# Gated cross-attention block with a quantized feed-forward: three global maxima turned by TensorE, unread matmuls ahead of the gate and down products, their first tiles worked together

## The chip, the cores and the metric

The kernel runs on one core of one Trainium2 (trn2) chip. The metric is the device time of one execution in microseconds (us), as the median of several runs; a time is better when it is lower. A change of 0.3% is about 5.7 us here.

## What is computed

The reference is a two-part transformer block on `x` of shape (4, 1024, 512): a gated cross-attention with 16 heads of 32 columns, and a gated feed-forward (512 to 1536 and back) whose weights and activations are rounded to integer grids. Only the second part matters for this change:

```python
def act_qdq(x):
    qmax = 32767.0
    scale = jnp.maximum(jnp.max(jnp.abs(x)) / qmax, 1e-12)
    return jnp.clip(jnp.round(x / scale), -qmax - 1.0, qmax) * scale

x = act_qdq(x)
up = act_qdq(x @ lpbq_dequant(w_up).T)
gate = act_qdq(x @ lpbq_dequant(w_gate).T)
sig = fixed_qdq_u16(jax.nn.sigmoid(gate))
gate = act_qdq(gate * sig)
o = act_qdq(gate * up)
return o @ lpbq_dequant(w_down).T
```

Every `act_qdq` takes one maximum over a whole tensor of 4096 rows, and nothing behind it can be rounded before that maximum is known. So the feed-forward is a row of stages with a global maximum between each two.

## The kernel before, in words

Five programs run side by side, one for each engine's queue: `sync_program` (SP, all DMAs but a few), `tensor_program` (PE), `scalar_program` (ACT), `vector_program` (DVE) and `gpsimd_program` (POOL). They meet at semaphores only. Each program is written out in order; what an engine does next is the next line of its program, and it waits there if a semaphore is not yet high enough.

The first part (up to about 998 us) is the attention, cut into steps by `all_steps`. The change touches one line of it: `aggregate` (L1391), which turns the statistics of the last batch's rows into means and variances. POOL makes the standard deviations from them (`deviation_2`, L1729), and DVE the largest normalized value of all rows, "x_row" (L1492).

A global maximum is made by `everywhere` (L1326). Each partition holds its own maximum in one column. DVE spreads that column over 32 columns (L1329), turns the four 32x32 blocks (L1332), and reduces the turned rows into four blocks of partitions (L1335): nine DVE instructions, and every partition then holds the largest value. The names are listed at L272. `quant_scale` (L1477) makes the scales from it.

Then come these stages of the feed-forward:

- **x tiles.** 32 tiles of 128 rows are centred, scaled and split into a high and a low fp16 part: `centre_x` (L1293) and `quant_x` (L1498) on DVE, `high_x` (L1147) on ACT, `low_x` (L1504) on DVE, and a transposing DMA into `x_hl` by `turn_x` (L680) on SP. The first 8 tiles are made before the gate product starts; the others beside it, at units given by `x_tile` (L203).
- **gate.** 48 units (4 column parts of 1024 rows, `cp`, by 12 weight tiles, `ot`). `project` (L984) computes one unit: two halves `h` of 512 columns, 12 matmuls each, into one of four PSUM tiles (`quad`). The first unit of each `cp` waits before each half for the four x tiles of that half. ACT copies a unit out (`evict`, L1153) into one of three `ev` buffers; DVE takes its largest absolute value and its largest value (L1513, L1517); SP stores it. Beside that DVE also makes the x tiles of the next `cp` and rounds the weights of up and down (`TILE_JOBS`), all in the order of the units.
- **up.** 48 units more, while ACT and DVE work on the sigmoid of the gate. Then "u_row", the maximum of up.
- **product maximum.** 48 pieces; ACT takes two absolute values of each (L1208, L1222), DVE multiplies and reduces (L1608). PE has nothing to do. Then "o_row".
- **down.** 8 chunks `ch` of 512 rows. For each chunk and each of 12 `ot` the second operands are made (`make_o`, L1632: `quantize_up` on ACT, `make_oq` on DVE, `high_o` on ACT, `low_o` on DVE). PE then computes four output tiles of a chunk one after the other (L1009 to L1028), 36 matmuls each: 12 `ot` by 3 products. DVE adds the residual (L1652) and SP stores the tile (L864). The 12 operands of the first chunk are made before any output; those of chunk `ch + 1` beside the four tiles of chunk `ch`, three for each (L1644, and on SP L859 for their loads).

Of the kernel before, what the change touches and what calls it, by code (L numbers as in the profile page):

```python
# [6 lines left out]
ALU = mybir.AluOpType  # L7
ACT = mybir.ActivationFunctionType
AX = mybir.AxisListType
F32 = mybir.dt.float32  # L10
# [257 lines left out]

ALL = 9
ALL_NO = {n: ALL * (k + 1) for k, n in enumerate(("w0", "x_row", "w1", "w2", "g_row", "s_row", "h_row", "u_row", "o_row"))}  # L272


R1, R2 = 9, 9
# [19 lines left out]
class Kernel:  # L295


    def __init__(self, nc, ctx, x, ctx_in, gx, gf, wg, wu, wd, cos_d, sin_d, id_d, bias_d, out):
# [34 lines left out]
        self.ymax = A("ymax", [128, NT], F32)  # L333
        self.red = A("red", [128, 12], F32)
        self.spread = A("spread", [128, 32], F32)
        self.turned = A("turned", [32, 128], F32)
        self.qs = A("qs", [128, 24], F32)
        self.wmx = A("wmx", [128, 12], F32)
# [90 lines left out]
        def sem(name):  # L429
            return ctx.enter_context(nc.semaphore(name))  # L430
# [27 lines left out]
        self.pe_prj, self.pe_down = sem("pe_prj"), sem("pe_down")  # L458
# [28 lines left out]
    def bank_release(self, use, half):  # L487

        n = UNIT[use] - 2
        while n >= 0:  # L490
            kind, *a = UNIT_USES[n]
            if kind == "max":
                return self.v_max, max_no(*a)
            if kind == "out":
                return (self.v_x2 if half else self.v_rec), a[0] + 1
            if kind == "turn":
                return self.v_lo, turn_no(*a, half)
            if half == 0:
                return self.v_wl, w_no(*a)
            n -= 2  # L500
        return None

    def w_buffer(self, m, k):

# [59 lines left out]


TODO = [(ch, ot) for ch in range(NCH) for ot in range(OT)]

# [4 lines left out]
def sync_program(e, K):  # L572
# [253 lines left out]
    def load_o(n):  # L826
        ch, ot = TODO[n]
        load_up(ot, slice(512 * ch, 512 * ch + 512), 512)
# [25 lines left out]
    for ch in range(NCH):  # L854
        for i in range(4):
            m = 4 * ch + i
            if m + 1 < NT:
                load_xr(m + 1)
            if ch + 1 < NCH:  # L859
                for n in range(OT * (ch + 1) + 3 * i, OT * (ch + 1) + 3 * i + 3):  # L860
                    if n + NUF < len(TODO):
                        load_o(n + NUF)
# [9 lines left out]
def tensor_program(e, K):  # L872
# [108 lines left out]
        before = st  # L981


    def project(k, W, cp):  # L984
        z = k % 4
        for h in range(2):
            c0 = 1024 * cp + 512 * h
            if h == 0 and k >= 4:
                e.wait_ge(K.a_ev, k - 3)
            if k < 48 and k % OT == 0:  # L990
                for j in range(NXS):
                    e.wait_ge(K.d_xt[j], 16 * (c0 // 512) + 16)
            terms = [(0, c, c) for c in range(CC)] + [(0, c, CC + c) for c in range(CC)] + [(1, c, c) for c in range(CC)]
            for n, (part, c, x) in enumerate(terms):
                mm = e.matmul(K.quad[z][:, 512 * h:512 * h + 512], W(part, c), K.x_hl[:, x, c0:c0 + 512], start=n == 0, stop=n == 11)  # L995
        mm.then_inc(K.pe_prj, 1)

    e.wait_ge(K.a_den, NHALF)
    e.wait_ge(K.a_num, NHALF)
    e.wait_ge(K.d_Wg, 32)  # L1000
    for cp in range(4):
        for ot in range(OT):
            project(12 * cp + ot, lambda part, c: K.Wg[part][:, ot, 128 * c:128 * c + 128], cp)
    for ot in range(OT):
        e.wait_ge(K.d_Wu[ot % 2], 32 * (ot // 2) + 32)
        for cp in range(4):
            project(48 + 4 * ot + cp, lambda part, c: K.Wu[ot % 2][part][:, c, :], cp)

    for ch in range(NCH):  # L1009
        k = ch % 2  # L1010
        for i in range(4):
            n = 4 * ch + i
            z = n % 8
            ps = K.quad[z // 2][:, 512 * (z % 2):512 * (z % 2) + 512]
            sl = slice(128 * i, 128 * i + 128)
            if n == 0:
                e.wait_ge(K.a_ev, 96)
                e.wait_ge(K.d_Wd, 128)
            if n >= 8:
                e.wait_ge(K.v_out, n - 7)  # L1020
            m = 0
            for ot in range(OT):
                if i == 0:
                    e.wait_ge(K.v_ol, OT * ch + ot + 1)
                for o, r in ((K.oh, 0), (K.ol, 0), (K.oh, 1)):
                    mm = e.matmul(ps, o[k][:, ot, sl], K.Wd[r][:, ot, :], start=m == 0, stop=m == 3 * OT - 1)  # L1026
                    m += 1
            mm.then_inc(K.pe_down, 1)  # L1028

# [225 lines left out]
def vector_program(e, K):  # L1255
# [69 lines left out]

    def everywhere(out, column, name):  # L1326

        n = ALL_NO[name] - ALL
# [75 lines left out]
    for st in STEPS:  # L1404
# [45 lines left out]
        if st.stats is not None:  # L1450
            p, qc, part = st.stats
            g, c = p % 4, slice(4 * qc, 4 * qc + 4)
            if part == 0:
                if (p, qc) == (NQ - 1, 1):
                    e.wait_ge(K.v_x2b, 1)
                else:
                    e.wait_ge(K.g_x2, 2 * p + qc + 1)
                for i in range(4 * qc, 4 * qc + 4):
                    e.bn_stats(K.st2[:, i, g, :], K.x2s[:, i, :]).then_inc(K.v_st2, 1)
            else:  # L1460
                o, op = (K.rmx, ALU.max) if part == 1 else (K.rmn, ALU.min)
                e.tensor_reduce(o[:, c, g], K.x2s[:, c, :], AX.X, op).then_inc(K.v_st2, 1)
# [178 lines left out]
    for ch in range(NCH):  # L1641
        for i in range(4):
            m = 4 * ch + i
            if ch + 1 < NCH:  # L1644
                for n in range(OT * (ch + 1) + 3 * i, OT * (ch + 1) + 3 * i + 3):
# [221 lines left out]
```

## Time and profile before

| | us |
|---|---|
| median of 3 runs (lowest, highest) | 1890.52 (1889.78, 1894.19) |
| the profiled execution, its time | 1895.78 |
| the profiled execution, its span (first to last instruction) | 1894.0 |
| PE busy, share of the span | 1680.0, 89% |
| DVE busy | 1498.3, 79% |
| ACT busy | 1184.7, 63% |
| POOL busy | 809.7, 43% |

Busy times are sums over stages with different limits, so the shares say little about one stage. Times in rows count from the first instruction of the span. A row of the timeline reads: start, duration, engine, line, operation, output tile <- input tiles, shape of output <- input, count, and in brackets how long the engine was idle before it and what ended that. SPq is the DMA queue that SP feeds; its rows are the issues of DMAs, not their transfers. PEld is the load of a matmul's stationary operand. PEclk is the granted clock of TensorE as a share of 2.4 GHz: 1.00 is 2.4 GHz, 0.50 is 1.2 GHz, values between are means over a stretch in which it changed.

### The profile page before, as it was taken

To read this page: it belongs to the slowest core of one execution; us is meant where nothing else is said; L and a number is where in the kernel's file an instruction comes from. 1 tells how busy PE (TensorE), PEld (TensorE's weight loads), DVE (VectorE), ACT (ScalarE), POOL (GpSimd) and SP (SyncE) were. 2 spreads that over 40 slices of the span, in tenths; PEclk is the share of its full clock that TensorE was granted. 3 is DMA by queue.
4 is the path that set the end of the run, shared out by engine and by line. 5 is a ranking of instruction groups with operands and counts; after the bars stand their busy time and mean duration, and the time that the engine had idled before them with its cause. 6 is when DMAs were issued, how large, how long until landed. Compare 5 with 4: busy or idle time off the path is not lost. (4 is left out here: it accounts for less than half of the span.)

```text
span 1894.0 us, 24954 instructions
## 1 busy us (share of the span) xinstructions
PE 1680.0 (89%) x8888; PEld 632.1 (33%) x8888; DVE 1498.3 (79%) x2140; ACT 1184.7 (63%) x1898; POOL 809.7 (43%) x442
## 2 busy tenths in 40 slices
PE   2899999999999999999985999999999920399999
PEld 0223333333333333333222444444444400144444
DVE  6899888888888887888845998968889999855551
ACT  3476777777777777777662332329896689744440
POOL 4488888978889888887630010110000000000000
PEclk9899999999999999999997999999999965699999
DMA  5576777656776667766454888749993469755552
GB/s 157 142 177 155 182 178 185 145 141 140 182 180 139 166 141 177 170 140 139 86 167 129 251 259 245 231 156 267 281 280 131 139 213 291 250 175 167 168 172 72
DMA packets 234044, 339.49 MB, mean 179 GB/s; under 512 B 74400, under 2 KB 153120, under 8 KB 225664
## 3 DMA queue, kind: packets, MB, share of 16 engines
q1 hardware_dynamic: 224992, 272.89, 48.2%
q0 software_dynamic: 8928, 65.02, 17.2%
q8 instruction: 70, 1.15, 0.3%
q14 instruction: 54, 0.44, 0.1%
HBM read 164.04 MB, written 92.41 MB: 135 GB/s over the span
## 5 line engine op out<-in xcount | busy, mean ns | idle before, releaser
L1074 ACT ACTIVATE P<-quad 128x512 f32<-128x512 f32 x1024 | 557.3, 599 | 231.4 <-PE quad L913 227.1
L1271 DVE TENSOR_REDUCE cm<-quad 128x1 f16<-128x1024 f32 x512 | 601.1, 1216 | 86.3 <-PE quad L901 85.0
L1792 POOL TENSOR_TENSOR Ps<-P,P 128x2048 f32<-128x2048 f32 x93 | 422.8, 4546 | 153.8 <-ACT P L1074 153.7
L913 PE MATMUL quad<-QA,KA 101*128 101x512 f16 x1024 | 352.8, 385 | 7.5 <-ACT P L1074 6.4
L901 PE MATMUL quad<-KA,QA 100*128 100x512 f16 x1024 | 328.0, 391 | 27.1 <-DVE wh L1379 6.6
L1026 PE MATMUL quad<-Wd,oh 128*128 128x512 f16 x768 | 231.2, 381 | 113.7 <-DVE ol L1630 113.7
L949 PE MATMUL quad<-P,cg 128*32 128x512 f32 x2048 | 273.6, 606 | 3.5 <-ACT numT L1111 0.6
L995 PE MATMUL quad<-x_hl,Wg 128*128 128x512 f16 x1152 | 251.7, 382 | 23.1 <-DMA x_hl<-xs 22.9
L995 PE MATMUL quad<-x_hl,Wu 128*128 128x512 f16 x1152 | 250.7, 381 | 2.1 <-DMA Wu<-wt_scratch 2.1
L1158 ACT ACTIVATE ev<-quad 128x1024 f32<-128x1024 f32 x96 | 97.3, 1015 | 151.7 <-PE quad L995 145.8
L913 PEld LDWEIGHTS quad<-QA,KA 101*128 101x128 f16 x1024 | 86.1, 97 | 299.9 <-ACT P L1074 208.5
L995 PEld LDWEIGHTS quad<-x_hl,Wg 128*128 128x128 f16 x1152 | 113.0, 98 | 161.6 <-issue 27.8
L995 PEld LDWEIGHTS quad<-x_hl,Wu 128*128 128x128 f16 x1152 | 113.0, 98 | 139.5 <-DMA Wu<-wt_scratch 2.8
L901 PEld LDWEIGHTS quad<-KA,QA 100*128 100x128 f16 x1024 | 98.7, 98 | 172.9 <-DVE cm L1271 38.3
L1513 DVE TENSOR_REDUCE mxt<-ev 128x1 f32<-128x1024 f32 x96 | 116.6, 1215 | 42.3 <-ACT ev L1158 41.7
L1026 PE MATMUL quad<-Wd,ol 128*128 128x512 f16 x384 | 146.3, 381 | 0.0
L1026 PEld LDWEIGHTS quad<-Wd,oh 128*128 128x128 f16 x768 | 75.3, 98 | 209.5 <-issue 111.8
L1183 ACT ACTIVATE sgm<-gq,qs 128x1024 f32<-128x1024 int16 x96 | 110.1, 1147 | 39.0 <-DVE sgq L1555 37.4
L1768 POOL TENSOR_TENSOR wq<-wl,wsc 128x512 f32<-128x512 f32 x36 | 37.8, 1051 | 221.1 <-DVE wl L1388 221.1
L1652 DVE SCALAR_TENSOR_TENSOR xr<-quad,qs,xr 128x512 f32<-128x512 f32 x32 | 24.0, 750 | 122.6 <-PE quad L1026 122.6
L979 PE MATMUL quad<-Ps,ones 128*32 128x512 f32 x776 | 101.0, 592 | 1.8 <-DMA Ps<-P 1.5
L1236 ACT ACTIVATE uq<-uf,qs 128x512 int16<-128x512 f32 x96 | 68.2, 711 | 53.8 <-DMA uf<-up_scratch 51.9
(149 smaller groups left out, 1847.8 us busy)
## 6 DMA issues: line engine op xcount, KB each, us to landing
Ps<-P POOLq DMA_DIRECT2D x62, 1024.0 KB, 7.9
gate_scratch<-ev SPq DMA_DIRECT2D x48, 512.0 KB, 3.2
gt<-gate_scratch SPq DMA_DIRECT2D x48, 512.0 KB, 5.7
up_scratch<-ev SPq DMA_DIRECT2D x48, 512.0 KB, 3.2
uf<-up_scratch SPq DMA_DIRECT2D x48, 512.0 KB, 5.1
uf<-up_scratch SPq DMA_DIRECT2D x96, 256.0 KB, 3.7
QA<-part_scratch SPq DMA_DIRECT2D x45, 256.0 KB
KA<-part_scratch SPq DMA_DIRECT2D x45, 256.0 KB
```

Source lines behind the costliest of these rows:

```text
L901: mm = e.matmul(K.bank(use, c), K.QA[p % 2][0:100, qc, h, q0:q0 + 128], K.KA[p % 2][0:100, h, 512 * c:512 * c + 512], start=True, stop=True)
L913: e.matmul(K.score[h % 2], K.KA[p % 2][0:101, h, 128 * kt:128 * kt + 128], K.QA[p % 2][0:101, qc, h, :], start=True, stop=True).then_inc(K ...
L949: mm = e.matmul(K.num[32 * h:32 * h + 32, :], K.cg[p % 3][:, kt, 32 * h:32 * h + 32], K.Pb[before.g % NP][:, h, :], start=kt == 0, stop=kt ...
L979: mm = e.matmul(K.den[32 * h:32 * h + 32, :], K.ones[:, :], K.Ps[n % 2 if hf == NHALF - 1 else n][:, h, :], start=n == 0, stop=n == (3 if ...
L995: mm = e.matmul(K.quad[z][:, 512 * h:512 * h + 512], W(part, c), K.x_hl[:, x, c0:c0 + 512], start=n == 0, stop=n == 11)
L1026: mm = e.matmul(ps, o[k][:, ot, sl], K.Wd[r][:, ot, :], start=m == 0, stop=m == 3 * OT - 1)
L1074: e.activation(K.Pb[pb][:, h, :], K.score[h % 2], ACT.Exp, scale=SCALE / (QPOW * KPOW)).then_inc(K.a_exp, 1)
L1158: e.activation(K.ev[k % NEV][:, :], K.quad[k % 4][:, :], ACT.Copy).then_inc(K.a_ev, 1)
L1183: e.activation(K.sgm[n % NSG][:, :], view(n), ACT.Sigmoid, scale=sg).then_inc(K.a_sig, 1)
L1271: e.tensor_reduce(cm[:, u:u + 1], K.quad[UNIT["max", hm, u] % 2][:, :], AX.X, ALU.max).then_inc(K.v_max, 1)
L1513: e.tensor_reduce(K.mxt[:, col:col + 1], K.ev[k % NEV][:, :], AX.X, ALU.max, apply_absolute_value=True).then_inc(K.v_mx, 1)
L1792: e.tensor_tensor(K.Ps[n][:, :, :], K.Pb[(st.g - 1) % NP][:, :, :], K.Pb[st.g % NP][:, :, :], ALU.add).then_inc(K.g_sum, 1)
```

## The change

- x_row, u_row and o_row are turned by TensorE: DVE spreads the column over 128 columns, PE transposes the 128x128 block into PSUM, DVE reduces that. The other six maxima stay as they were.
- Ahead of the gate product PE runs 24 matmuls into `quad[3]`, and ahead of down 12, whose results nobody reads (`warm`). Those ahead of the gate wait for the first x tile's low part; those ahead of down stand behind the transpose of o_row.
- The first four gate units run all their first halves, then all their second halves.
- The first four output tiles of down run together: for each `ot`, all four tiles.
- The 12 operands of down's chunk 1 (and their loads, on SP) come before the first output instead of three before each of the first four. The chunks behind it stay as they were.
- The first four of the last batch's eight `bn_aggr` stand before the statistics of its second half.

```diff
-ALL = 9
-ALL_NO = {n: ALL * (k + 1) for k, n in enumerate(("w0", "x_row", "w1", "w2", "g_row", "s_row", "h_row", "u_row", "o_row"))}
+BY_TENSOR = ("x_row", "u_row", "o_row")
+ALL_NO = {}
+for name in ALL_ORDER:
+    ALL_NO[name] = max(ALL_NO.values(), default=0) + (2 if name in BY_TENSOR else 9)
...
+    def all_bank(self, name):
+        return self.quad[2 if name == "x_row" else 0][:, 0:128]
...
+def operands_beside(ch, i):
+    if ch + 1 == NCH or ch == 0 and i > 0:
+        return range(0)
+    return range(OT, 2 * OT) if ch == 0 else range(OT * (ch + 1) + 3 * i, OT * (ch + 1) + 3 * i + 3)
...
@@ tensor_program @@
-    def project(k, W, cp):
+    def project(k, W, cp, h):
...
+    def turn_column(name):
+        e.wait_ge(K.v_all, ALL_NO[name] - 1)
+        e.transpose(K.all_bank(name), K.column[:, :], ident).then_inc(K.pe_all, 1)
+    def warm(W, count):
+        for n in range(count):
+            e.matmul(K.quad[3][:, 0:512], W[:, 0, 0:128], W[:, 1, 0:512], start=True, stop=True)
+    turn_column("x_row")
     e.wait_ge(K.a_den, NHALF)
     e.wait_ge(K.a_num, NHALF)
     e.wait_ge(K.d_Wg, 32)
+    e.wait_ge(K.v_xlo, 1)
+    warm(K.Wg[0], 24)
+    gate_tiles = [(cp, ot) for cp in range(4) for ot in range(OT)]
+    halves = [(t, h) for h in range(2) for t in gate_tiles[:4]] + [(t, h) for t in gate_tiles[4:] for h in range(2)]
+    for (cp, ot), h in halves:
+        project(12 * cp + ot, lambda part, c: K.Wg[part][:, ot, 128 * c:128 * c + 128], cp, h)
...
+    e.wait_ge(K.a_ev, 96)
+    turn_column("u_row")
+    e.wait_ge(K.d_Wd, 128)
+    turn_column("o_row")
+    warm(K.Wd[0], 12)
...
+    for ot in range(OT):
         for i in range(4):
+            down(0, i, ot)
+    for ch in range(1, NCH):
+        for i in range(4):
             for ot in range(OT):
+                down(ch, i, ot)
@@ vector_program, everywhere @@
+        if name in BY_TENSOR:
+            e.tensor_reduce(K.column[:, :], column.to_broadcast([128, 128]).unsqueeze(2), AX.X, ALU.max).then_inc(K.v_all, 1)
+            e.wait_ge(K.pe_all, BY_TENSOR.index(name) + 1)
+            e.tensor_reduce(out, K.all_bank(name), AX.X, ALU.max).then_inc(K.v_all, 1)
+            return
@@ vector_program, aggregate and stats @@
-        for i in range(8):
+        for i in range(4 if b == B - 1 else 0, 8):
...
                 if (p, qc) == (NQ - 1, 1):
+                    e.wait_ge(K.v_st2, 12 * p + 6)
+                    for i in range(4):
+                        e.bn_aggr(K.mv2[:, 8 * (B - 1) + i, :], K.st2[:, i, :, :].rearrange("p g s -> p (g s)")).then_inc(K.v_mv2, 1)
                     e.wait_ge(K.v_x2b, 1)
@@ vector_program and sync_program, the outputs of down @@
-            if ch + 1 < NCH:
-                for n in range(OT * (ch + 1) + 3 * i, OT * (ch + 1) + 3 * i + 3):
-                    make_o(n)
+            for n in operands_beside(ch, i):
+                make_o(n)
```

## Rows read from the trace of the kernel before

**Rows 1.** The page's busy times, PE alone.
```profile
PE 1680.0 (89%) x8888; PEld 632.1 (33%) x8888; DVE 1498.3 (79%) x2140; ACT 1184.7 (63%) x1898; POOL 809.7 (43%) x442
```
**Rows 2.** Busy time by stretch: length, PE, PEld, DVE, ACT, POOL, PEclk, DMA share, GB/s.
```profile
998.00:1020.00 22.00, 0.32 (x1) 0.14 (x2) 15.37 (x48) 4.67 (x8) 3.30 (x9) 0.56 0.39 82
1020.00:1025.00 5.00, 4.89 (x12) 1.51 (x11) 0.69 (x1) 0.26 (x1) 0.00 (x0) 0.53 0.92 184
1025.00:1060.00 35.00, 34.97 (x163) 15.87 (x164) 27.16 (x37) 9.32 (x12) 0.00 (x0) 1.00 0.79 240
...
1533.00:1626.00 93.00, 0.00 (x0) 0.00 (x0) 85.29 (x133) 87.75 (x87) 0.00 (x0) 0.50 0.89 287
1626.00:1649.00 23.00, 10.20 (x33) 2.74 (x33) 20.81 (x48) 17.09 (x28) 0.00 (x0) 0.72 0.61 189
```
**Rows 3.** Timeline, the start of the gate product.
```profile
1011.35 0.69 DVE L1509 SCALAR_TENSOR_TENSOR xs<-xf,xs 128x512 f16<-128x512 f32 x1 [0.36 <-ACT xs L1151]
...
1019.68 10.68 PE L995 MATMUL quad<-x_hl,Wg 128*128 128x512 f16 x36 [21.96 <-DMA x_hl<-xs]
...
1025.00 5.09 PEld L995 LDWEIGHTS quad<-x_hl,Wg 128*128 128x128 f16 x25 [0.94 <-issue]
...
1028.87 1.22 DVE L1513 TENSOR_REDUCE mxt<-ev 128x1 f32<-128x1024 f32 x1 [7.88 <-ACT ev L1158]
```
**Rows 4.** Line L682 from 1010 to 1026 us: issue durations in ns, issue to landing.
```profile
L682 SPq DMA_TRANSPOSE x_hl<-xs x8: 1307/1332/1357, 1012.1 to 1021.7; - x8
...
DMA to landing us min/median/max: 3.2/3.4/3.4
```
**Rows 5.** Waits of DVE, 1030 to 1143 us: total, times, longest.
```profile
DVE mxt L1513 <- ACT ev L1158: 14.2, 7, 7.9
```
**Rows 6.** Timeline, x tiles 15 and 23 on their way, and PE's wait.
```profile
1079.95 0.68 DVE L1509 SCALAR_TENSOR_TENSOR xs<-xf,xs 128x512 f16<-128x512 f32 x1
1081.03 1.47 SPq L682 DMA_TRANSPOSE x_hl<-xs  x1
...
1142.14 0.68 DVE L1509 SCALAR_TENSOR_TENSOR xs<-xf,xs 128x512 f16<-128x512 f32 x1
...
1145.27 1.95 SPq L682 DMA_TRANSPOSE x_hl<-xs  x1
...
1150.44 1.89 PE L995 MATMUL quad<-x_hl,Wg 128*128 128x512 f16 x8 [0.94 <-DMA x_hl<-xs]
```
**Rows 7.** Timeline, around u_row.
```profile
1530.43 4.82 ACT L1208 ACTIVATE ol<-gq 128x1024 int16<-128x1024 int16 x5
...
1533.19 0.19 DVE L1329 TENSOR_REDUCE spread<-red 128x32 f32<-128x32 f32 x1
...
1535.57 0.21 DVE L1479 TENSOR_SCALAR qs<-red,qs 128x1 f32<-128x1 f32 x1
...
1536.40 1.15 ACT L1222 ACTIVATE oh<-uf,qs 128x1024 int16<-128x1024 f32 x1 [1.14 <-DVE qs L1485]
```
**Rows 8.** A PE transpose's rows (ns), and a DVE reduction of 192 columns.
```profile
L886 PE MATMUL quad<-ident,t x256: 270/273/477, 17.3 to 886.0; 128*128 128x128 f32 x128
...
L1353 DVE TENSOR_REDUCE wmx<-wsc x2: 294/294/294, 1070.5 to 1185.6; 128x1 f32<-128x192 f32 x2
```
**Rows 9.** Timeline around o_row and down's first operands, and the chain's last row.
```profile
1630.02 0.19 DVE L1329 TENSOR_REDUCE spread<-red 128x32 f32<-128x32 f32 x1
...
1635.63 0.59 PE L1026 MATMUL quad<-Wd,oh 128*128 128x512 f16 x1 [110.48 <-DVE ol L1630]
...
1649.01 241.71 PE quad L1026 x1119
```
**Rows 10.** PE alone by stretch in down's start: length, PE, PEclk, DMA share, GB/s.
```profile
1639.00:1639.50 0.50, 0.50 (x4) 0.92 0.56 135
...
1640.00:1645.00 5.00, 3.36 (x13) 1.00 0.72 217
```
**Rows 11.** Timeline, the eight `bn_aggr` of the last batch.
```profile
1001.50 1.11 DVE L1398 BATCH_NORM_AGGREGATE mv<-st 128x2 f32<-128x24 f32 x8
```

More of the change, by code:

```diff
@@ L267, in wsc_no @@
     return n if m == 0 else 4 + 6 * (m - 1) + n
-ALL = 9
-ALL_NO = {n: ALL * (k + 1) for k, n in enumerate(("w0", "x_row", "w1", "w2", "g_row", "s_row", "h_row", "u_row", "o_row"))}
+ALL_ORDER = ("w0", "x_row", "w1", "w2", "g_row", "s_row", "h_row", "u_row", "o_row")
+BY_TENSOR = ("x_row", "u_row", "o_row")
+ALL_NO = {}
+for name in ALL_ORDER:
+    ALL_NO[name] = max(ALL_NO.values(), default=0) + (2 if name in BY_TENSOR else 9)
 R1, R2 = 9, 9
@@ L335, in __init__ @@
         self.spread = A("spread", [128, 32], F32)
+        self.column = A("column", [128, 128], F32)
         self.turned = A("turned", [32, 128], F32)
@@ L457, in __init__ @@
         self.pe_tden, self.pe_tnum, self.pe_wturn = sem("pe_tden"), sem("pe_tnum"), sem("pe_wturn")
-        self.pe_prj, self.pe_down = sem("pe_prj"), sem("pe_down")
+        self.pe_prj, self.pe_down, self.pe_all = sem("pe_prj"), sem("pe_down"), sem("pe_all")
         self.a_tg, self.a_bias = sem("a_tg"), sem("a_bias")
@@ L858, in sync_program @@
                 load_xr(m + 1)
-            if ch + 1 < NCH:
-                for n in range(OT * (ch + 1) + 3 * i, OT * (ch + 1) + 3 * i + 3):
-                    if n + NUF < len(TODO):
-                        load_o(n + NUF)
+            for n in operands_beside(ch, i):
+                if n + NUF < len(TODO):
+                    load_o(n + NUF)
             e.wait_ge(K.v_out, m + 1)
@@ L981, in tensor_program @@
         before = st
-    def project(k, W, cp):
+    def project(k, W, cp, h):
         z = k % 4
[L986 to L996, printed above, removed]
+        c0 = 1024 * cp + 512 * h
+        if h == 0 and k >= 4:
+            e.wait_ge(K.a_ev, k - 3)
+        if k < 48 and k % OT == 0:
+            for j in range(NXS):
+                e.wait_ge(K.d_xt[j], 16 * (c0 // 512) + 16)
+        terms = [(0, c, c) for c in range(CC)] + [(0, c, CC + c) for c in range(CC)] + [(1, c, c) for c in range(CC)]
+        for n, (part, c, x) in enumerate(terms):
+            mm = e.matmul(K.quad[z][:, 512 * h:512 * h + 512], W(part, c), K.x_hl[:, x, c0:c0 + 512], start=n == 0, stop=n == 11)
+        if h == 1:
+            mm.then_inc(K.pe_prj, 1)
+    def turn_column(name):
[5 more added lines that the diff above has]
+    turn_column("x_row")
     e.wait_ge(K.a_den, NHALF)
@@ L1000, in tensor_program @@
     e.wait_ge(K.d_Wg, 32)
-    for cp in range(4):
-        for ot in range(OT):
-            project(12 * cp + ot, lambda part, c: K.Wg[part][:, ot, 128 * c:128 * c + 128], cp)
+    e.wait_ge(K.v_xlo, 1)
[4 more added lines that the diff above has]
+        project(12 * cp + ot, lambda part, c: K.Wg[part][:, ot, 128 * c:128 * c + 128], cp, h)
     for ot in range(OT):
@@ L1006, in tensor_program, with down @@
         for cp in range(4):
-            project(48 + 4 * ot + cp, lambda part, c: K.Wu[ot % 2][part][:, c, :], cp)
-    for ch in range(NCH):
-        k = ch % 2
-        for i in range(4):
[L1012 to L1021, printed above, removed]
-            for ot in range(OT):
[L1023 to L1028, printed above, removed]
+            for h in range(2):
+                project(48 + 4 * ot + cp, lambda part, c: K.Wu[ot % 2][part][:, c, :], cp, h)
+    e.wait_ge(K.a_ev, 96)
[3 more added lines that the diff above has]
+    warm(K.Wd[0], 12)
+    def down(ch, i, ot):
+        n = 4 * ch + i
+        k, z = ch % 2, n % 8
+        ps = K.quad[z // 2][:, 512 * (z % 2):512 * (z % 2) + 512]
+        sl = slice(128 * i, 128 * i + 128)
+        if n >= 8 and ot == 0:
+            e.wait_ge(K.v_out, n - 7)
+        if i == 0:
+            e.wait_ge(K.v_ol, OT * ch + ot + 1)
+        for m, (o, r) in enumerate(((K.oh, 0), (K.ol, 0), (K.oh, 1))):
+            mm = e.matmul(ps, o[k][:, ot, sl], K.Wd[r][:, ot, :], start=ot == m == 0, stop=ot == OT - 1 and m == 2)
+        if ot == OT - 1:
+            mm.then_inc(K.pe_down, 1)
+    for ot in range(OT):
+        for i in range(4):
+            down(0, i, ot)
+    for ch in range(1, NCH):
+        for i in range(4):
+            for ot in range(OT):
+                down(ch, i, ot)
 def scalar_program(e, K):
@@ L1326, in everywhere @@
     def everywhere(out, column, name):
-        n = ALL_NO[name] - ALL
+        if name in BY_TENSOR:
[3 more added lines that the diff above has]
+            return
+        n = ALL_NO[name] - 9
         e.tensor_reduce(K.spread[:, :], column.to_broadcast([128, 32]).unsqueeze(2), AX.X, ALU.max).then_inc(K.v_all, 1)
@@ L1643, in vector_program @@
             m = 4 * ch + i
-            if ch + 1 < NCH:
-                for n in range(OT * (ch + 1) + 3 * i, OT * (ch + 1) + 3 * i + 3):
-                    make_o(n)
+            for n in operands_beside(ch, i):
+                make_o(n)
             z = m % 8
```

## The prediction

> **What bounds the kernel.** I start with the page's busy times. PE is busy for 89% of the span [rows 1], so the question is where PE stands still or runs slowly. The busy times by stretch show three such places, all at stage borders [rows 2]: from 998 to 1020 us PE does nothing while the x maximum is found and the first x tiles are made; from 1020 to 1025 us it works at a granted clock of about half; from 1533 to 1649 us it first has nothing to do (the product maximum, where DVE and ACT are over 90% busy) and then does 33 matmuls in 23 us, at half clock to begin with. In between, PE is full: 34.97 of 35 us.
>
> Next, the timeline of the gate's start [rows 3]. The first matmul comes at 1019.68, released by the DMA that turns the x tiles. Twelve matmuls take until 1024.8 (0.43 us each, the 1.2 GHz level), and from 1025.00 one takes half of that. The x tiles come in a row: eight issues of 1.33 us on SP's queue, each landed 3.4 us later [rows 4]. The fourth lets half 0 start, the eighth half 1 (1021.7 + 3.3 = 1025.0).
>
> Last, the chain of waits ends with 241.71 us of PE alone [rows 9]: 1119 down matmuls from 1649.01 to 1890.72, 0.216 us each, 2.4 GHz throughout. Before that, down's first tile crawls: its operands come every 1.22 us (eleven between 1635.63 and 1649.01 [rows 9]) and PE has three matmuls, 0.65 us, for each.
>
> **Part 1: maxima.** The nine DVE instructions take 2.38 us (1533.19 to 1535.57 [rows 7]; x_row and o_row look the same). The new way has no row. Its pieces: a DVE reduction of 128 columns, about 0.25 us (192 take 0.294 [rows 8]), twice; a PE transpose, 0.27 us at full clock and 0.48 at half [rows 8], and PE is idle long before each of the three, so half; a weight load and two hand-offs, some 0.3 us. Sum 1.3 us, saving **1.05 us** each. Bounds: no hand-offs and a fast PE, 0.77 us, saves 1.6; with each piece slow, 1.7 us, saves 0.7. PE and its queue are free at all three: nothing else of PE stands behind these transposes that could run earlier.
>
> For u_row the saving counts only if ACT can use it. ACT's previous work ends at 1535.25 and it then waits until 1536.40 for the scale [rows 7]: room for 1.15 us, so 1.05 passes on. From there the product stage is a relay of ACT, DVE and loads that ACT's progress releases, so it moves as a whole.
>
> **Part 2: the gate.** x tiles, their DMAs and the unread matmuls all move with x_row. The unread ones start when the first low part is done, 1012.04 [rows 3] less 1.05: 1011.0. At the half clock for 5.0 us as in this start [rows 3], 24 of them take 12 x 0.43 + 12 x 0.216 = 7.7 us and end at 1018.8; where the clock rises after 3.4 us, as in down (1635.63 to 1639.0 [rows 9, 10]), at 1018.1. Half 0's x tiles land at 1018.6. So the gate starts at **1018.7**, at full clock. It then has 48 matmuls, 10.4 us, that need only the first four x tiles; the others land at 1024, well inside. Before, PE stood at 1025.0 with 12 matmuls done, which at full clock is a start at 1022.4. PE gains **3.7 us**.
>
> Can the others follow? The first unit is now complete after 60 matmuls, at 1031.7, and with 1.25 us for the copy DVE begins it at 1032.9 instead of 1028.87 [rows 3]: **4.0 us later**. DVE had 14.2 - 7.9 = 6.3 us of waiting in its next 21 units [rows 5], and some 1 us in gaps too short to be listed. Without these it reaches the last x tile of the third quarter (tile 23) 6.3 + 1 - 4.0 = 3.3 us earlier than 1142.14 [rows 6], less about 0.4 for its longer hand-offs with POOL and ACT. This matters, since PE waited for that very tile before (0.94 us at 1150.44, its DMA issued at 1145.27 behind SP's weight stores [rows 6]). So the gate's gain is what DVE gains, not PE's 3.7: **2.9 us**. Tile 15 is the other narrow place: its low part ends at 1080.6 as before, lands 3.4 us later at 1084.0, and PE now wants it at 1083.5. Behind tile 23 all moves alike, and up, with PE full and ACT and DVE starting from the gate's maximum, too. Bounds: 3.7 (DVE is no limit) and 0 (DVE loses all its slack).
>
> **Part 3: down.** In the old time, o_row's spread at 1630.02 [rows 9] now reaches PE at 1630.4, the transpose ends at 1631.0, and the 12 unread matmuls follow at half clock. They end between 1635.3 (clock up after 3.4 us) and 1636.1 (after 5.0). The first operand is ready at 1635.63 - 1.05 = 1634.6, so the unread ones end last: down starts at **1635.7**. Four tiles together give PE 12 matmuls, 2.59 us, per operand that comes every 1.22 us: after the first it never starves. All 1152 matmuls take 248.8 us at 0.216. Before, PE ended at 1890.72, which is a start at 1641.9. Gain **6.2 us**, o_row's saving in it. Bounds: 5.8, and 7.3 if PE could start with the first operand.
>
> Part 4: the operands of chunk 1 ahead of the outputs. Twelve more at 1.22 us are done at about 1663, their loads issued on SP ahead of the first output's store; chunk 1 starts at 1635.7 + 31.1 = 1666.8. So they are in time, and without this edit they would be late, since the four outputs now come together at the end of chunk 0. What stands behind: the fourth output needs a residual buffer that the first store frees, some 5 us on SP's queue, and DVE waits there with chunk 2's operands behind it; but chunk 2 starts only at 1697.9. Cost: nothing.
>
> Part 5: four `bn_aggr`, half of 1.11 us [rows 11], move from behind the second half's statistics to ahead of them, in the same DVE queue on the same chain: nothing either way, within 0.1 us.
>
> **Sum.** 2.9 + 1.05 + 6.2 = **10.1 us**. The profiled execution, 1895.78, would become 1885.7. It lies 5.3 us above the median of the runs shown, 1890.52; from the median the same subtraction gives **1880.4**.
>
> **Rivals.**
>
> *The gate's gain is lost to DVE.* If the longer hand-offs eat the 6.3 us, tile 23 lands when it did, and the gate gains nothing: 10.1 - 2.9 = 7.2, giving 1883.3. For it: DVE is full from unit 14 on and PE already waited for tile 23 [rows 6]. Against: the waiting of rows 5 is real slack. Chance 0.15.
>
> *The unread matmuls don't raise the clock* (the change doesn't do what it says). Then the gate starts at 1018.6 with 5 us at half clock, PE gains 1.4 and DVE about 0.7; down starts at 1636.1 and loses 1.7 to 2.5 us to the clock, gaining 3.7. Sum 0.7 + 1.05 + 3.7 = 5.5, giving 1885.0. Against: they are matmuls of the same size as those under which the clock rose in both starts. Chance 0.08.
>
> *The clock falls back in down's first chunk* (the other side). PE now goes round four PSUM banks, three matmuls in each. If that let the clock drop, each of the 144 matmuls of the chunk would cost 0.21 us more, 30 us in all: 1880.4 + 30 = 1910. It decides from (10.1 + 5.7) / 0.21 = 75 slow matmuls. Against: from 1640 to 1645 PE was busy for 3.36 of 5 us, in bursts of three, and the clock stayed at 1.00 [rows 10]; the new order has fewer pauses. The Trainium skill ("TensorE: Matmul & The Clock Gate", section "A second HAM failure mode: psum-queue depth-cycling") tells of a kernel with N=512 in which cycling through PSUM banks left small pauses between groups of matmuls and the clock went up and down; by that rule this rival would hold, and rows 10 speak against it. Chance 0.04.
>
> **The numbers.** My forecast, with all parts inside their bounds, has the chance 0.73, and 1880.4 is its value. Its best end is 3.7 + 1.6 + 7.3 = 12.6, or 1877.9; its worst 0.5 + 0.7 + 5.8 = 7.0, or 1883.5. With 1 us for the median's own scatter at the lower end, and up to the edge of the second rival at the upper, the range is 1876.5 to 1885.5; outside it lie the last rival, half of the second and a few hundredths. A measurement can tell about 0.3%, 5.7 us, from no change. Faster by more: the forecast (0.72 of its 0.73) and most of the first rival (0.10), 0.82. Within: the rest of these and the second rival, 0.14. Slower: 0.04.
>
> **What would show it.** In the profile of the changed kernel: PE's first gate matmul near 1018.7 at a PEclk of 1.00; four copies by ACT from 1031.7 on, 2.6 us apart; a wait of PE for an x tile near 1147, about as long as before; u_row's and o_row's stretches 1.3 us long; down's first matmul at full clock with no pause of PE in chunk 0, and the last row of the chain some 249 us long. It would be wrong if DVE's tile 23 came no earlier than 1142, if the clock were at 0.50 in either start, or if PE waited for operands at chunk 1 or 2.

## The result, and the profile after

The changed kernel takes 1881.89 us (median of 6 runs, 1877.91 to 1885.22), the kernel before 1892.83 in the same job: a ratio of 0.9947 with an interval of 0.9931 to 0.9962, so 10.0 us faster. Measured twice more, beside the kernel before each time, it gave 0.9943 and 0.9946. Over all runs of the study the medians are 1891.84 (50 runs of before) and 1881.83 (16 of the change).

Single executions scatter by 3 to 5 us to either side. The profiled one of before (1895.78) is longer than each of these 50, that of the change (1877.91, span 1876.1) the shortest of its 16, so the 17.9 us between the two spans are not the change. To see where the time went I cut each profiled execution at the first reduction of x_row, g_row, u_row and o_row (`red<-` in the timeline) and did the same in every later run. The cuts are read to 0.1 us, so a stage is good to about 0.1. In us:

| profiled execution | attention | gate | up | product | down |
|---|---|---|---|---|---|
| before | 1007.1 | 268.9 | 256.9 | 96.8 | 264.2 |
| before, a second one | 1005.9 | 268.8 | 255.3 | 96.4 | 264.2 |
| changed | 1004.4 | 266.7 | 253.1 | 95.2 | 256.8 |
| changed, a second one | 1005.6 | 266.7 | 254.4 | 95.5 | 258.5 |
| changed, a third one | 1005.2 | 266.6 | 254.4 | 96.0 | 258.1 |
| mean difference | (1.4) | **2.3** | (2.2) | **1.1** | **6.4** |

Gate, product and down repeat within about 1.7 us and differ by 9.8 us together, where the medians differ by 10.0. Attention and up, hardly or not touched by the change, scatter by more (up from 253 to 257 over all fourteen executions, see the last section).

The page's busy times, to [rows 1]:

```profile
PE 1682.4 (90%) x8927; PEld 635.5 (34%) x8927; DVE 1492.9 (80%) x2119; ACT 1184.3 (63%) x1898; POOL 809.8 (43%) x442
```

PE has 39 matmuls more (36 unread, three transposes), DVE 21 instructions fewer.

Busy times by stretch, to [rows 2]:

```profile
1008.00:1012.00 4.00, 3.76 (x10) 1.41 (x11) 3.48 (x8) 1.77 (x3) 0.00 (x0) 0.54 0.65 125
1012.00:1016.00 4.00, 3.51 (x18) 1.42 (x16) 2.87 (x5) 1.67 (x4) 0.00 (x0) 1.00 1.01 192
1015.00:1055.00 40.00, 39.51 (x184) 17.82 (x183) 25.99 (x35) 10.33 (x13) 0.00 (x0) 1.00 0.81 215
...
1524.00:1616.00 92.00, 0.45 (x1) 0.18 (x1) 84.26 (x128) 87.99 (x87) 0.00 (x0) 0.50 0.89 291
1619.00:1624.00 5.00, 4.03 (x13) 1.68 (x14) 3.93 (x14) 2.56 (x5) 0.00 (x0) 0.63 0.50 157
1624.00:1630.00 6.00, 6.00 (x29) 2.76 (x29) 5.41 (x10) 6.00 (x12) 0.00 (x0) 1.00 0.59 182
1630.00:1655.00 25.00, 25.00 (x118) 11.34 (x116) 21.01 (x39) 21.71 (x36) 0.00 (x0) 1.00 0.64 199
```

In this execution the half clock (0.54 and 0.63) falls on unread matmuls. From the first real one on PE is full at 1.00, in the gate and in down, where 23 us held 33 matmuls before.

The timeline of the gate's start, to [rows 3] and the maxima of [rows 7]:

```profile
1004.59 0.29 DVE L1366 TENSOR_REDUCE column<-red 128x128 f32<-128x128 f32 x1
...
1004.94 0.47 PE L1015 MATMUL quad<-ident,column 128*128 128x128 f32 x1 [9.83 <-DVE column L1366]
1005.45 0.29 DVE L1368 TENSOR_REDUCE red<-quad 128x1 f32<-128x128 f32 x1 [0.57 <-PE quad L1015]
1005.77 0.15 DVE L1539 TENSOR_SCALAR qs<-red 128x1 f32<-128x1 f32 x1
...
1008.24 7.03 PE L1020 MATMUL quad<-Wg 128*128 128x512 f16 x24 [2.83 <-DVE xs L1555]
1015.77 17.43 PE L1009 MATMUL quad<-x_hl,Wg 128*128 128x512 f16 x80 [0.49 <-DMA x_hl<-xs]
1028.91 1.02 ACT L1195 ACTIVATE ev<-quad 128x1024 f32<-128x1024 f32 x1 [12.57 <-PE quad L1009]
1029.97 1.22 DVE L1559 TENSOR_REDUCE mxt<-ev 128x1 f32<-128x1024 f32 x1 [12.90 <-ACT ev L1195]
```

The maximum takes from 1004.59 to 1005.77, 1.18 us. The unread matmuls end in time, the first real one follows the x tiles, and DVE's first unit comes 25.6 us behind the start of x_row (it was 21.75).

PE's waits from 1000 to 1280 us, and the timeline of x tile 23, to [rows 6]:

```profile
PE quad L1009 <- DMA x_hl<-xs: 3.0, 4, 1.3
```

```profile
1135.82 2.00 SPq L686 DMA_DIRECT2D wt_scratch<-wh  x2
1137.86 0.93 SPq L671 DMA_DIRECT2D wl<-in_L_ffn_w_down_dram  x2
1138.83 0.43 SPq L765 DMA_DIRECT2D gate_scratch<-ev  x1
1139.31 1.78 SPq L698 DMA_TRANSPOSE x_hl<-xs  x1
...
1144.81 5.55 PE L1009 MATMUL quad<-x_hl,Wg 128*128 128x512 f16 x25 [1.25 <-DMA x_hl<-xs]
...
1207.82 4.48 PE L1009 MATMUL quad<-x_hl,Wg 128*128 128x512 f16 x20 [0.69 <-DMA x_hl<-xs]
```

The tile's low part was done at 1136.85, but its DMA stands behind two weight stores, two loads and a gate store on SP and is issued 2.5 us later. (Before it was the same: done at 1142.82, issued at 1145.27.) The other waits are 0.49 at the start, 0.56 at 1081.24 (tile 15) and 0.69 at 1207.82 (tile 31).

The timeline around u_row (to [rows 7]):

```profile
1524.31 0.29 DVE L1366 TENSOR_REDUCE column<-red 128x128 f32<-128x128 f32 x1
...
1525.56 0.21 DVE L1525 TENSOR_SCALAR qs<-red,qs 128x1 f32<-128x1 f32 x1
...
1526.38 1.15 ACT L1259 ACTIVATE oh<-uf,qs 128x1024 int16<-128x1024 f32 x1
```

and around o_row, with the chain's last piece (to [rows 9]):

```profile
1619.54 0.29 DVE L1366 TENSOR_REDUCE column<-red 128x128 f32<-128x128 f32 x1
...
1619.97 0.45 PE L1015 MATMUL quad<-ident,column 128*128 128x128 f32 x1 [94.78 <-DVE column L1366]
1620.21 3.98 PE L1020 MATMUL quad<-Wd 128*128 128x512 f16 x12
...
1623.44 0.43 DVE L1676 TENSOR_TENSOR ol<-oq,oh 128x512 f16<-128x512 int16 x1
...
1624.03 0.38 PE L1054 MATMUL quad<-Wd,oh 128*128 128x512 f16 x1
...
1624.20 248.65 PE quad L1054 x1152
```

In this execution the unread matmuls end just as the first operand does (1623.87), and PE then runs 1152 matmuls without a pause to the end.

### The profile page after: what moved, and what is told of

It reads as the page before. It is cut to its first block and busy times, and to the rows that moved or that the text cites. A ratio compares the mean times of both kernels' runs of the same rounds, so it can differ in the third digit from the quotient of the medians.

```text
span 1876.1 us, 25013 instructions
## 1 busy us (share of the span) xinstructions
PE 1682.4 (90%) x8927; PEld 635.5 (34%) x8927; DVE 1492.9 (80%) x2119; ACT 1184.3 (63%) x1898; POOL 809.8 (43%) x442
## 5 line engine op out<-in xcount | busy, mean ns | idle before, releaser
L1009 PE MATMUL quad<-x_hl,Wu 128*128 128x512 f16 x1152 | 248.8, 379 | 0.0
```

## Experiments

Each is the changed kernel with one edit, unless it says otherwise; stages are cut as above.

**The two kernels again.** No edit; to learn how far a stage repeats.

> The changed kernel again, for how far its stages repeat. Stages are cut at the first reduction of x_row, g_row, u_row and o_row; in the two profiles they took, before and after: attention 1007.1 and 1004.4 us, gate 268.9 and 266.6, up 256.9 and 253.1, product 96.8 and 95.2, down 264.2 and 256.8. My theory: the change made 2.3 (gate) + 1.6 (product) + 7.4 (down) = 11.3 us of the 17.9 between the two profiles; the 2.7 of the attention and the 3.8 of up are scatter between executions. Then gate, product and down repeat within 0.5 us, and the ratio to before is 0.994 to 0.995. Rival: up's 3.8 us belong to the change; then the ratio is 0.992.

> The kernel before again, for its up stage. In its profile PE waited 2.08 us there for one weight transpose from memory, at 1398.97, and then worked at a granted clock of 0.83 for a slice of 10 us; the changed kernel's profile has neither. My theory: this is scatter; up takes 253 us here, without the wait, and gate 268.9, product 96.8, down 264.2 repeat within 0.5. Rival: the old gate order makes that wait; then it comes again and up takes 257.

Measured: the rows of the table above. Of the three stages that were to repeat within 0.5 us, down did not: 258.5 against 256.8. For the kernel before, the expected 253 us in up were missed: PE waited 2.31 and 0.73 us for up's weights again, and up took 255.3. But the wait doesn't belong to the old gate order, since the change's second and third execution waited 1.74 and 1.80 us for these weights too. The timeline of the second execution of the change:

```profile
1623.04 5.33 PE L1020 MATMUL quad<-Wd 128*128 128x512 f16 x12
1626.27 0.42 DVE L1676 TENSOR_TENSOR ol<-oq,oh 128x512 f16<-128x512 int16 x1
...
1628.16 0.63 PE L1054 MATMUL quad<-Wd,oh 128*128 128x512 f16 x1
```

All twelve unread matmuls ran at half clock here, and the first operand, done at 1626.69, waited 1.5 us for them. So their number is right only where the clock rises early.

**The old order of the gate's first units**, the unread matmuls kept.

```diff
-    halves = [(t, h) for h in range(2) for t in gate_tiles[:4]] + [(t, h) for t in gate_tiles[4:] for h in range(2)]
+    halves = [(t, h) for t in gate_tiles for h in range(2)]
```

> The changed kernel with the first four gate units in the old order (both halves of one unit, then the next). PE starts as early and at full clock, but after 12 matmuls it waits for x tiles 4 to 7, so its work stands 2.7 us later than in the changed kernel; DVE gets its first unit 5 us earlier. My theory (the gate's end is set by DVE and the x tiles that it makes, PE's start counts in part): gate takes 267.8 us, 1.2 more than in the changed kernel. Rival A, PE's start counts in full: 269.3. Rival B, the order doesn't matter, since DVE's earlier start makes up for it: 266.6 or less. Other stages as in the changed kernel.

Measured: gate 269.8, worse than the theory said by 2.0 us. The timeline and PE's busy time by stretch (length, PE, PEclk, DMA share, GB/s):

```profile
1014.12 2.75 PE L1009 MATMUL quad<-x_hl,Wg 128*128 128x512 f16 x12 [0.24 <-DMA x_hl<-xs]
1019.53 10.70 PE L1009 MATMUL quad<-x_hl,Wg 128*128 128x512 f16 x41 [2.66 <-DMA x_hl<-xs]
```

```profile
1017.00:1019.50 2.50, 0.00 (x0) 1.00 0.91 170
1019.50:1021.00 1.50, 1.47 (x7) 0.93 0.75 285
1021.00:1024.00 3.00, 3.00 (x9) 0.50 0.02 5
1024.00:1027.00 3.00, 3.00 (x15) 0.96 0.51 175
```

PE waited 2.66 us for the second four x tiles, as expected. What nobody expected is that the clock, still 1.00 through the wait, fell to 0.50 about 1.3 us after work went on, for 3.4 us. That costs another 1.7 us and makes up most of the difference: the total lies beyond rival A's 269.3, but without the fall of the clock it would be 268.1, near the theory's 267.8. In the gate stage of this one execution the new order is worth 3.1 us, 1.4 of them without the fall of the clock. The median, 1882.63 (ratio 0.9946, 0.9932 to 0.9959), does not show this: the mean of the 5 runs is 0.6 us above the change's, uncertain by 2.0, which leaves room for the 1.4 but not for the 3.1 in every execution.

**No unread matmuls ahead of the gate.** Tried twice, the second time beside a third run of the change, since the first median did not show what its gate stage did.

```diff
-    warm(K.Wg[0], 24)
```

> The changed kernel without the 24 unread matmuls ahead of the gate. My theory: the first gate matmuls run at 1.2 GHz for 3.4 to 5 us, so PE and DVE's first unit are 1.7 to 2.5 us later, DVE carries that on to the x tiles of the next quarters, and gate takes 268.7 us, 2.1 more than the changed kernel. Rival: PE's waits for x tiles in the gate (0.6, 1.3 and 0.7 us) take the delay up; gate takes 266.6 to 267.2. Other stages as in the changed kernel.

> The change without the 24 unread matmuls ahead of the gate, a second time, beside the change itself on the same chip. Its first profile had a gate stage of 270.0 us against 266.7, yet its median of 1882.9 was that of the change, and its attention 1003.3 us against 1004.4 and 1005.6. Theory (the gate's loss is real, the attention's length is scatter from one execution to the next): gate 270.0 again (269.5 to 270.3), attention anywhere from 1002.7 to 1006, median 3 us above the change's in this job (1.5 to 4.5). Rival (something behind or ahead of the gate gives the loss back in this kernel): gate 270.0, attention 1003.3 or less again, or up below 253, and the medians within 1 us of each other.

> The changed kernel a third time, for its stages beside the run above: gate 266.7 (266.3 to 267.0), up 253 to 256 by whether a load of up's weights is late, product 95.2 to 95.6, down 256.8 to 258.5 by how soon the clock rises under the unread matmuls, attention 1002.7 to 1006; median 1882 (1880 to 1884).

Measured: gate 270.0 (1.3 more than the theory's 268.7) and 268.0, against 266.6 in the change, whose third execution came as expected but for the product stage (96.0). PE by stretch in the second run without them:

```profile
1019.00:1020.00 1.00, 1.00 (x4) 0.50 1.00 196
1020.00:1021.00 1.00, 1.00 (x4) 0.58 0.94 183
1021.00:1022.00 1.00, 1.00 (x6) 1.00 1.03 191
```

From its first gate matmul (1017.20) the half clock lasts 3.6 us; in the first of the two runs it lasted 5.9. So the expected 270.0 was missed the second time, and so were the 3 us between the medians: what is saved depends on when the clock rises, 1.3 to 3.4 us in the gate stage. The medians are 1882.86 and 1882.34, and 1881.65 for the change in the second job; over 11 and 16 runs the means are 1882.3 and 1881.8. With a scatter of 2.4 and 2.1 us per run the difference of 0.5 is uncertain by 1.8. A gain of 3.4 us in the usual execution is excluded by that, one of 1.3 isn't. The up stage was no shorter in these runs (255.6 and 256.3), nor was any stage behind the gate more than 0.5 us under the changed kernel's lowest, so nothing was seen to give the gain back; why the medians show less than the gate stages remains open, here and for the order. One thing the stages do show: with the order alone or the unread matmuls alone the gate took 268.0 to 270.0 us, hardly less or even more than the 268.9 before the change.

**The old order of down's first tiles**, operands ahead kept.

```diff
-    for ot in range(OT):
-        for i in range(4):
-            down(0, i, ot)
-    for ch in range(1, NCH):
+    for ch in range(NCH):
```

> The changed kernel with down's first four output tiles one after the other again (operands of chunk 1 still ahead of the outputs). My theory: the first tile goes at the pace of the operands, eleven times 1.22 us, so 31 tiles of 7.77 us stand behind 13.8 us: PE ends 6.0 us later than with four tiles together. Down takes 263 to 264 us, where the changed kernel took 256.8 to 258.5 in four profiles. Rival: working four together only moves the wait to chunk 1; then down takes 257 to 258.5. Gate, 266.7, and product, 95.4, as in the changed kernel.

Measured: down 263.1, as expected; 1886.27 us (ratio 0.9968, 0.9956 to 0.998). PE's waits from 1600 to 1700 us, and the longest piece of the chain:

```profile
PE quad L1054 <- DVE ol L1673: 4.2, 11, 0.4
```

```profile
1636.86 241.71 PE quad L1054 x1119
```

It is the piece of before, 241.71 us for 1119 matmuls: without the four tiles together, the first tile again starves eleven times.

**Chunk 1's operands not ahead.**

```diff
-    if ch + 1 == NCH or ch == 0 and i > 0:
+    if ch + 1 == NCH:
...
-    return range(OT, 2 * OT) if ch == 0 else range(OT * (ch + 1) + 3 * i, OT * (ch + 1) + 3 * i + 3)
+    return range(OT * (ch + 1) + 3 * i, OT * (ch + 1) + 3 * i + 3)
```

> The changed kernel with the operands of down's chunk 1 beside the first four outputs again, three before each. My theory: the four outputs of chunk 0 now come at its end, so the operands 15 to 23 are made only from there on, nine times 1.22 us with three outputs of 0.75 us between them; PE waits in chunk 1 and ends about 4.3 us later: down takes 261 us (259.5 to 263). Rival, chunk 1 needs its operands no earlier than they come either way: 257 to 258.5.

Measured: down 263.4, above the expected range; 1886.0 us (10 runs, ratio 0.997, 0.9961 to 0.998). PE's waits, and the chain's longest pieces in down:

```profile
PE quad L1054 <- DVE ol L1676: 4.0, 6, 1.2
```

```profile
1627.66 29.36 PE quad L1054 x135
1670.92 210.62 PE quad L1054 x975
```

Between the two pieces the chain runs through chunk 1's operands and their loads. Six waits, 4.0 us. Most of the rest over the theory's 261 is the clock: the unread matmuls took 5.1 us here as in the second execution of the change, against whose 258.5 the loss is 4.9 (4.3 expected). The rival is refuted. Working the four tiles together and making operands ahead belong together: with either one left out and all else kept, down gains 0.8 (no operands ahead) and 1.1 us (old order) on the kernel before, instead of 6.4.

**No unread matmuls ahead of down.**

```diff
-    warm(K.Wd[0], 12)
```

> The changed kernel without the 12 unread matmuls ahead of down. In its two profiles of the changed kernel these took 3.8 and 5.1 us; with 3.8 the first down matmul came with its first operand, with 5.1 it came 1.3 us behind it. My theory: without them it comes with its operand, at 1.2 GHz for 3.4 to 5.9 us (as seen at the gate's start in different runs), which costs 1.7 to 2.9 us: down takes 258.5 to 259.7. So the unread matmuls are worth 0 to 2.9 us here. Rival, the clock is up anyway because of the transpose for o_row: down takes 256.8 without scatter.

Measured: down 258.6; 1881.74 us (ratio 0.9945, 0.9932 to 0.9958), the change's own time.

```profile
1628.21 0.61 PE L1053 MATMUL quad<-Wd,oh 128*128 128x512 f16 x1 [3.50 <-DVE ol L1675]
...
1632.33 0.38 PE L1053 MATMUL quad<-Wd,ol 128*128 128x512 f16 x1
```

PE starts with the first operand, at half clock for about 4 us. Against 256.8, 258.5 and 258.1 with the unread ones they are worth 0.1 to 1.8 us (four other runs that leave down as changed took 257.1 to 258.0): what they give in clock they mostly take in time, and no median shows them.

**All maxima by DVE again.** The unread matmuls ahead of down wait for o_row's spread.

```diff
-BY_TENSOR = ("x_row", "u_row", "o_row")
+BY_TENSOR = ()
...
-    turn_column("x_row")
...
-    turn_column("u_row")
...
-    turn_column("o_row")
+    e.wait_ge(K.v_all, ALL_NO["o_row"] - 8)
```

> The change with all nine maxima turned by DVE again; the unread matmuls ahead of down now wait for o_row's spread. Stages are cut at the first reduction of x_row, g_row, u_row, o_row and at the span's end; the changed kernel had 266.7 and 266.7 us for the gate, 95.2 and 95.5 for the product maximum, 256.8 and 258.5 for down. Theory (each TensorE-turned maximum saves about 1.1 to 1.2 us and all three pass on): gate 267.9 (267.6 to 268.2), product 96.5 (96.2 to 96.8), down 258.0 to 258.6 (the first operand 1.1 later; where the unread matmuls took 5.1 us they had hidden part of it), so 3.0 to 3.5 us in all and a time near 1885. Rival (a maximum's saving is lost to the next wait): that stage stays at 266.7, or 95.3, or 256.8.

Measured: gate 268.2, product 97.4, down 258.0; 1884.01 us (ratio 0.9968, 0.9956 to 0.9981). The gate loses 1.6, the product 1.4 to 2.2, more than the 1.1 to 1.2 expected of it. One execution of that stage scatters too much to tell: with u_row turned by TensorE it took 94.8 to 96.3 us in eleven profiles, 95.6 in the mean, and with DVE's u_row 96.4, 96.8 and 97.4. Down, at the expectation's lower end, loses 1.2 against one execution of the change and gains 0.1 to 0.5 on the other two:

```profile
1629.71 5.28 PE L1020 MATMUL quad<-Wd 128*128 128x512 f16 x12 [105.73 <-DVE spread L1369]
...
1634.41 0.43 DVE L1674 TENSOR_TENSOR ol<-oq,oh 128x512 f16<-128x512 int16 x1
1634.90 0.49 PE L1052 MATMUL quad<-Wd,oh 128*128 128x512 f16 x1
```

The unread ones take 5.28 us and end with the slower operand. So o_row's saving counts only where the clock rises early under them; elsewhere they cover it.

**SP turns an x tile first in its unit.** An addition: tile 23's DMA waited behind weight transfers.

```diff
         for ot in range(OT):
+            if x_tile(12 * cp + ot, 3) is not None:
+                turn_x(x_tile(12 * cp + ot, 3))
             for job in TILE_JOBS.get(12 * cp + ot, []):
...
-            if x_tile(12 * cp + ot, 3) is not None:
-                turn_x(x_tile(12 * cp + ot, 3))
```

> The changed kernel with SP issuing each later x tile's turning DMA first in its unit, ahead of that unit's weight stores, weight loads and gate store (before it stood behind them: tile 23 was ready at 1136.85 and issued at 1139.31). My theory: the gate's end is set by when tiles 15, 23 and 31 land, so PE's waits for them (0.4 to 0.6, 1.25 to 1.35 and 0.7 us) go, and gate takes 264.3 to 265.2 us instead of 266.7. Rival: the transfers themselves are late behind other DMA work, or the later stores hold ACT's buffers: 266.7 or more.

Measured: gate 264.3, as expected; 1878.76 us (5 runs, 1878.48 to 1879.06; ratio 0.9932, 0.9919 to 0.9944). PE's waits from 1000 to 1250 us:

```profile
PE quad L1009 <- DMA x_hl<-xs: 0.6, 1, 0.6
```

Only tile 15's wait is left. Tile 23's low part comes at the same time as in the change, 132.4 us behind the first reduction of x_row (132.5 there), but its DMA is issued at once and also lands sooner: 3.1 us from its issue, where behind the weight stores it took 5.4. So the rest of the gate's gain was held by SP's queue, with DVE's part of the path as it was.

**Two more on top of that**: a third buffer for up's weights, and 8 of 22 unread matmuls ahead of o_row's transpose.

```diff
-        if ot >= 2:
-            e.wait_ge(K.pe_prj, 48 + 4 * (ot - 2) + 4)
+        if ot >= 3:
+            e.wait_ge(K.pe_prj, 48 + 4 * (ot - 3) + 4)
...
-        if ot + 1 < OT:
-            load_wu(ot + 1)
+        if ot + 2 < OT:
+            load_wu(ot + 2)
...
+    e.wait_ge(K.v_pmax, 46)
+    warm(K.Wd[0], 8)
     turn_column("o_row")
-    warm(K.Wd[0], 12)
+    warm(K.Wd[0], 14)
```

> The change with SP issuing an x tile's turn first in its unit (as in the run before of that kind), and two things more: a third buffer for the weights of up, so that their transposing loads are issued one weight tile (20.7 us) earlier, and 8 of 22 unread matmuls put ahead of o_row's transpose, behind the 46th of 48 product pieces. Theory: gate 264.3 (264.0 to 264.6) as before; up 253.0 (252.6 to 253.5), since TensorE's waits for these weights, 0 to 3.3 us in the profiles so far, go and nothing else lies there; down 256.5 (256.2 to 256.9), its first matmul as soon as its first operand, 4.6 us behind o_row's first reduction, at full clock. Against 1878.8 us for the turn-first kernel, 255.87 for up and 257.11 for down: a time of 1875.4 (1874 to 1877). Rival A (the waits for the weights come from the DMA queues, not from the two buffers): up stays at 255 to 256, time 1878. Rival B (the clock falls between the two groups of unread matmuls, or the first group delays the transpose): down 258 or more.

Measured: gate 264.6, up 253.5, product 96.0, down 256.7; 1877.88 us (ratio 0.9932, 0.9918 to 0.9945). PE by stretch around o_row:

```profile
1618.00:1620.00 2.00, 1.46 (x5) 0.50 0.48 175
1620.00:1622.00 2.00, 2.00 (x8) 0.77 0.58 179
1622.00:1624.00 2.00, 2.00 (x10) 1.00 0.23 87
```

PE had no wait in up, and the clock was up before down's first matmul; both stages are near the lowest seen. The time misses the expected 1875.4 (1874 to 1877), although the three stages fell into their ranges: it is 0.9 us below the run with the turns first, less than the two scatter, so a gain over that is not shown. Both beat the change, by 3 to 4 us.

## Why the prediction was right

The forecast, 1880.4, is 1.5 us below the median, and the terms of its sum, 2.9 + 1.05 + 6.2, stand against 2.3 + 1.1 + 6.4 measured. The sum fits better than its terms: a gate gain 0.6 too high and a down gain 0.2 too low partly cancel, and that is luck. Most of the 1.5 us is the base: 1890.52 was the median of three runs, where 50 give 1891.84.

Not every part is shown in the kernel's time. Against the change's 1881.83, leaving out the new order of down costs 4.4 us in the median, the operands ahead 4.2, TensorE's maxima 2.2 (a mean of 3.1, uncertain by 2.3). For the gate's order and both groups of unread matmuls the medians differ by 1 us or less; what they are worth is read from the gate and down stages of single profiles only.

**Maxima.** 1.05 us each was predicted; the stretch from spread to scale fell from 2.38 to 1.18 (x_row), 1.25 (u_row) and 1.24 us (o_row), saving 1.1 to 1.2. The pieces are those of the sum: for x_row 0.29, 0.47 at half clock, 0.29 and hand-offs of 0.13 us together (the prediction took 0.3, from no row). u_row's passed on: ACT starts 2.07 us behind the spread's start, it was 3.21, and the product stage was longer with DVE's u_row in all three profiles that have it.

**Gate.** Counted from the first reduction of x_row, the prediction had the first real matmul at 11.6 us and DVE's first unit at 25.8; they came at 11.4 and 25.6. ACT's first four copies came 2.6 us apart, from 24.5 us on (24.6 predicted). PE was to gain 3.7, and gained 3.9: 11.4 against a start that before was worth 15.3. It then loses 0.56 at tile 15 (called the other narrow place), 1.25 at tile 23 where 0.94 were lost before, and 0.69 at tile 31: 3.9 - 0.56 - 0.31 - 0.69 = 2.3, the gate's gain. At tile 23 the prediction still held: its low part came 3.2 us earlier and PE went on 140.4 us behind x_row's first reduction, 143.3 before, 2.9 earlier as predicted (2.4 to 2.9 over the other executions). The step that failed is "behind tile 23 all moves alike": at tile 31 PE's wait was none and 0.31 us in the two executions before, and is now 0.69, 0.73 and 0.39. In the profiled pair tile 31's DMA was issued 2.9 us earlier too, but took 4.9 us to land instead of 4.3; why it took longer is open. And "the gate's gain is what DVE gains" is only half of the path: behind DVE the tile's DMA stood behind SP's weight transfers for 2.5 us, before as after, and moving it ahead took the waits at tiles 23 and 31 away with DVE's program unchanged.

One reading of the trace before was too general: "in between, PE is full" rests on one stretch of 35 us. In the up stage of that execution PE stood for 2.08 us and worked at half clock for 3.4 us behind that (last section). The change doesn't touch it, so the sum doesn't suffer.

**Down.** Predicted: start 5.9 us behind o_row's first reduction, set by the unread matmuls, gain 6.2. Measured: 4.7, 6.0 and 5.9 us behind it; gain 7.4, 5.7 and 6.1. The bound of 7.3 "if PE could start with the first operand" is the first of these; in the two others the clock was up 5.7 and 4.9 us behind the first unread matmul. The 6.2 came out because the executions fall on both sides of it. The second one also shows a sign that the prediction had called wrong, the clock at 0.50 in a start: for the first 0.6 us of down. In the profile shown all of down ran at full clock without a pause, 248.65 us for 1152 matmuls (248.8).

**Operands ahead.** "Without this edit they would be late": shown, 4.9 us in the stage. The residual buffers kept DVE waiting for 4.2 us in two waits, some 5 predicted, and no operand of chunk 2 was late for it: PE had no wait in down.

**`bn_aggr`.** Two groups of four, 0.62 us each, for 1.11 in one. A shift of 0.1 us can't be seen in an attention stage that scatters from 1002.7 to 1009.2, and no run leaves this edit out: its effect is not shown.

**The rivals.** The first (the gate's gain is lost to DVE) would have left a gate of 268.9: refuted, though 0.6 of its 2.9 us came about at tile 31. The second (the clock isn't raised) is refuted by a PEclk of 1.00 at the gate's start, where the runs without unread matmuls began at 0.50; at down's start it is half true in executions like the second. The third (the clock falls back in down's first chunk) is refuted: 1.00 from 1624 to 1655 with PE full. The rule it drew on, of the Trainium skill ("TensorE: Matmul & The Clock Gate", section "A second HAM failure mode: psum-queue depth-cycling"), is that in a kernel with N=512 cycling through PSUM banks left small pauses between groups of matmuls and the clock went up and down; here four banks with three matmuls each left no pause.

## What to carry to other kernels

Where a global maximum or a slow first operand stops TensorE, put the real work in an order in which the first pieces of data serve as many matmuls as possible; then look at who delivers the next pieces, since they are now wanted earlier (chunk 1's operands here, tiles 23 and 31 in the gate). Work that doesn't matter, until just before the real work, can raise the clock as well, but it gave less here: 1.3 to 3.4 us in the gate stage and 0.1 to 1.8 in down, not seen in the medians. A wait that "DVE" seems to cause may sit in a DMA queue: compare the time at which the data was ready with the time at which its DMA was issued. And cut every profiled execution into stages before believing a difference of spans: 8 of the 17.9 us here belonged to the executions, not to the kernels.

## What was not expected of the hardware

**Some pauses of more than 2 us cost more than themselves.** In the fourteen profiled executions PE paused 43 times for 0.3 to 1.80 us while it waited for an x tile or for weights, from 1025 us to the end of up; the granted clock was 1.00 in the 8 us behind each. The six longer pauses, the fifth at the gate's start:

| pause, us | execution | granted clock behind it |
|---|---|---|
| 2.08 | before, up | 0.50 for 3.4 us |
| 2.08 | no unread ahead of gate, up | 1.00 |
| 2.31 | before, second, up | 0.50 for 3.4 us |
| 2.33 | no unread ahead of gate, second, up | 1.00 |
| 2.66 | old gate order, gate | 0.50 for 3.4 us |
| 2.81 | old gate order, up | 0.50 for 3.4 us, 3.0 of it at work |

(Lengths are worked out from the mean PEclk of stretches of 1 to 3 us.) The clock fell between 0.4 us before and 1.3 us after PE was at work again, and the price is some 1.7 us on top of the pause. These waits are most of why up took 253 to 257 us: with two buffers the weights' transposing loads made PE wait 0 to 3.7 us in all, from one execution to the next, in both kernels. Less these waits and the slow stretches, up is 252.4 to 253.5 us in twelve of the fourteen executions; in the other two (before, second; old gate order) some 2 us of the lost time didn't reach the stage's end. With three buffers there was no such wait, in one execution; but the first execution of the change had none either, with two.

**The time to full clock varies.** From the first matmul after a long rest (the single transposes ahead not counted) to a PEclk of 1.00 it took 2.5 us (down, first execution of the change), 3.5 and 4.6 (gate, first and third), 3.6 and 5.9 (gate, no unread ones) and 5.7 (down, second execution). A fixed number of unread matmuls is therefore too many in one execution and too few in the next; beginning them ahead of the maximum, as the last experiment did, took them off the path: there the first operand was done at 1623.35 and PE began at 1623.40.
